# Two 16-head attentions: softmax sums on DVE, sharing on POOL, transposes of whole 128-column chunks

## The reference

```python
# first layer (A): 16 heads of 16, keys and values from the 77 context tokens
e = exp(s - max(s)); p = e / (exp(-m) * 0 + 1.0 + sum(e))     # softmax_one: one more column of weight 1
x = x + tanh(g_xattn[0]) * ((p @ v).heads_joined @ Wp + bp)
# second layer (B): a feed-forward whose two weight matrices are first quantised
scale = max(abs(w)) / 127
wq = clip(round(w / scale), -128, 127) * scale;  w = w + (wq - w)
# seventh layer (G): the same attention, with a bias per head, query and key, and a key mask
attn = q @ k.T * scale + bias;  attn = where(mask, -inf, attn)
x = x + tanh(g_xattn[3]) * ((softmax(attn) @ v).heads_joined @ o_w + o_b)
```

## Time and profile before

| what | value |
|---|---|
| median of 3 runs | 1403.33 us (1400.31 to 1404.64) |
| profiled execution, its own time | 1398.52 us |
| its span, first to last instruction | 1396.5 us |
| PE busy | 1121.6 us (80%) |
| DVE busy | 819.8 us (59%) |
| ACT busy | 580.9 us (42%) |
| POOL busy | 314.9 us (23%) |
| mean granted PE clock | 0.886 of full |

### The profile page before, as it was taken

One profiled execution on the slowest core, in us unless ns is written; L12 is line 12 of the kernel. 1 busy time (PEld: TensorE's weight loads), 2 busy tenths in 40 slices (PEclk: granted clock), 3 DMA queues, 4 the chain that ended last, 5 costly groups with the idle time before them and its releaser, 6 DMA issues.

```text
span 1396.5 us, 22604 instructions
## 1 busy us (share of the span) xinstructions
PE 1121.6 (80%) x8519; PEld 844.9 (60%) x8519; DVE 819.8 (59%) x2107; ACT 580.9 (42%) x1448; POOL 314.9 (23%) x283
## 2 busy tenths in 40 slices
PE   4998799986989897957998899997888752996730
PEld 3666588884447545734666788884666731785530
DVE  5899722248558467972636764556888450552463
ACT  2665433342448535712415313225898440342210
POOL 0009134200435103420010000000000036435266
PEclk9899899995899899988999999997999655898775
DMA  9300054400000003000000720001221023444253
GB/s 316 129 2 2 19 160 131 125 1 0 1 0 2 1 1 121 2 12 12 1 23 2 202 90 1 0 1 37 74 74 38 24 84 105 135 136 115 92 152 118
DMA packets 59841, 88.74 MB, mean 64 GB/s; under 512 B 21315, under 2 KB 50749, under 8 KB 56925
## 3 DMA queue, kind: packets, MB, share of 16 engines
q1 hardware_dynamic: 52301, 67.05, 14.8%
q0 software_dynamic: 7440, 20.33, 5.3%
HBM read 60.60 MB, written 26.76 MB: 63 GB/s over the span
## 4 chain that ended last, share of the span: by engine, by line
PE 52%; DVE 19%; issue 11%; ACT 8%; POOL 4%; another core or an unknown queue 4%; DMA 1%; SPq 0%; POOLq 0%; DVEq 0%; ACTq 0%
PE ps L2571 5%; PE ps L1405 4%; PE ps L1939 4%; PE ps L800 4%; PE ps L813 4%; ACT work L487 2%; POOL pack_F L2830 2%; PE ps L2585 2%; PE ps L1950 2%; PE ps L380 2%; DVE dpack L1731 1%; PE ps L366 1%; DVE work L628 1%; ACT work L494 1%
## 5 line engine op out<-in xcount | busy, mean ns | idle before, releaser
L2822 POOL DMA_INDIRECT hall<-hall_rows,tile_idx x47 | 44.7, 950 | 381.0 <-DVE tile_idx L2728 328.2
L2571 PE MATMUL ps<-big,work 128*128 x316 | 89.2, 408 | 24.9 <-ACT work L2629 16.3
L1905 POOL TENSOR_TENSOR work<-work 128x512 f32<-128x512 f32 x64 | 65.1, 1039 | 143.6 <-DVE work L1753 143.6
L380 PE MATMUL ps<-work,hall 78*32 78x128 f32 (+1 forms) x2048 | 71.7, 282 | 17.4 <-ACT work L494 15.9
L2732 DVE TENSOR_TENSOR work<-work,ps 128x128 f32<-128x128 f32 x79 | 22.9, 290 | 106.4 <-ACT work L2633 51.0
L366 PE MATMUL ps<-pack_const,work 128*78 128x128 f32 (+1 forms) x512 | 73.8, 290 | 9.1 <-DVEq L593 9.1
L2571 PEld LDWEIGHTS ps<-big,work 128*128 128x128 f32 x316 | 58.1, 205 | 32.6 <-issue 27.4
L380 PEld LDWEIGHTS ps<-work,hall 78*32 78x32 f32 (+1 forms) x2048 | 53.9, 112 | 38.5 <-ACT work L494 33.2
L628 DVE RECIPROCAL work<-ps 128x128 f32<-128x128 f32 x64 | 60.8, 950 | 24.8 <-PE ps L380 24.8
L1855 ACT ACTIVATE work<-ps,work 128x256 f32<-128x256 f32 x128 | 58.9, 476 | 38.0 <-DVE work L1748 37.9
L487 ACT ACTIVATE work<-work 128x77 f32<-128x77 f32 x256 | 67.3, 347 | 14.3 <-DVE work L615 13.5
(11 more groups left out here) (515 smaller groups left out, 2644.9 us busy)
## 6 DMA issues: line engine op xcount, KB each, us to landing
expert_rows<-work SPq DMA_DIRECT2D x39, 256.0 KB
masked_bias<-hall SPq DMA_DIRECT2D x8, 1232.0 KB, 5.2
dpack<-masked_bias SPq DMA_DIRECT2D x8, 1232.0 KB, 6.2
hall<-in_fside SPq DMA_DIRECT2D x8, 616.0 KB, 7.4
dpack<-in_pack_D SPq DMA_DIRECT2D x1, 4115.0 KB, 15.7
big<-in_w SPq DMA_DIRECT2D x4, 1024.0 KB, 11.9
big<-in_pack_B SPq DMA_DIRECT2D x1, 2052.0 KB, 10.3
pack_F<-in_pack_F SPq DMA_DIRECT2D x1, 2052.0 KB, 22.4
```

What stands on the lines that cost most here:

```text
L380: mm = nc.tensor.matmul(ps[j * HB32:(j + 1) * HB32, 4, half:half + P], lhsT, A["pT"][0:SK[L], u % 2, h * P:(h + 1) * P], start=g == 0, sto ...
L2571: mm = nc.tensor.matmul(ps[:, GU_B[j % 2], 0:2 * INTER], MW["xT"][:, j % 2, c * P:(c + 1) * P], big[:, bass.ds(at + c * 2 * INTER, 2 * INT ...
```

## The change

The order of work is now given by round g, 0 to 17, in all lists; k = 2g + c counts units. Part by part:

- **Sums on DVE.** `weigh_sum(k)` sums the weights of each head over the free axis (128x8 out of 624 in A, 616 in G) and takes the reciprocal of the eight sums. `normalise` goes, and with it the 128x128 reciprocal and the product on DVE, and half of the matmuls of `weigh_v`, those with the ones.
- **Shares on POOL.** A new list `heads16_pool`: `share(k)` multiplies the weights by the reciprocals. In G `below_max(k)` subtracts the maximum on POOL, so that ACT can do all eight heads in one exponential. `add_bias(g)` adds gate times bias to x on POOL, once for each tile, and `update` on DVE keeps two instructions, with the projection read from PSUM.
- **Flat transposes.** The 624 or 616 weights of a unit are turned in five chunks of up to 128 columns, without regard to heads. The values are laid out to match (`vflat`, eight blocks): at the start PE spreads them with 16 products against shifted copies of the identity (`spread_values`), and DVE copies two banks of PSUM (`take_spread`). `take_pT` copies 640 columns; ACT copies the output to SBUF (`take_o`).
- **Order.** Queries, scores and q are done half by half. DVE takes the first unit's sum ahead of the update of x.
- **Quantisation.** POOL does the two maxima over partitions in round 6 (`ffn_scale_pool`), between the second share of that round and its bias. From round 9 on, each round has one of eight parts of 512 columns: three scalings (`ffn_round_pool`) and two products (`ffn_error_pool`), five instructions in place of six. `ffn_max_dve` stands in rounds 4 and 5 of DVE, `ffn_inv_dve` in round 8.
- POOL's mask work for G, which was behind the quantisation, is now behind all of A's list. D's semaphores have other names.

The core of the diff; its first loop over g is PE's list:

```diff
-            def weigh_v(i, u):
-                for half in (0, D):
-                    for g in range(2):
-                        for j in range(HPG):
-                            lhsT = KV["count"][0:SK[L], b, g, :] if half else KV["vpad"][0:SK[L], b, c * HPC + h, :]
...
+            def turn_p(k, xs):
+                pe.wait_ge(s("pn_ready"), k + 1 + done(L, "pn_ready"))
...
+                for r in range(NCHUNK):
+                    n = chunk_rows(L, r)
+                    mm = nc.tensor.transpose(ps[0:n, PT_BANK + r // 4, r % 4 * P:(r % 4 + 1) * P],
+                                             flat_weights(L, k)[:, r * P:r * P + n], ident)
...
+            def weigh_v(k):
...
+                for e in range(2):
+                    for j in range(HPG):
+                        r, g = VBLOCKS[2 * j + e]
+                        n = chunk_rows(L, r)
+                        mm = nc.tensor.matmul(ps[g * HB32:(g + 1) * HB32, 4, 0:P], KV["vflat"][0:n, 2 * j + e, m, :],
+                                              A["pT"][0:n, k % 2, r * P:(r + 1) * P], start=e == 0, stop=e == 1,
...
+            for g in range(NG16 + 2):
+                if n < HT:
+                    queries(n, co)
+                if g >= 2:
+                    weigh_v(2 * (g - 2) + 1)
+                if 1 <= g <= NG16:
+                    turn_p(2 * (g - 1), min(2 + g // 2, HT))
+                if g >= 2:
+                    project(g - 2)
+                if g % 2 and n + 1 < HT:
+                    turn_x(n + 1)
+                if 1 <= g <= NG16:
+                    weigh_v(2 * (g - 1))
+                if g + 1 < NG16:
+                    scores(g + 1)
+                if 1 <= g <= NG16:
+                    turn_p(2 * (g - 1) + 1, min(2 + (g + 1) // 2, HT))
...
+            def exps(k):
...
+                else:
+                    act.wait_ge(s("below_ready"), k + 1)
+                    nc.scalar.activation(p, sub, ACT.Exp).then_inc(s("p_ready"), 1)
```

The loop of POOL's list:

```diff
+            for g in range(NG16 + 1):
+                if g:
+                    share(2 * (g - 1))
+                if L == "A" and g >= QUANT_AT:
+                    ffn_round_pool(pool, g - QUANT_AT)
+                if L == "G" and g < NG16:
+                    below_max(2 * g)
+                if g:
+                    share(2 * (g - 1) + 1)
+                if L == "A" and g == QUANT_AT - 3:
+                    ffn_scale_pool(pool)
+                if L == "A" and g >= QUANT_AT:
+                    ffn_error_pool(pool, g - QUANT_AT)
+                if L == "G" and g < NG16:
+                    below_max(2 * g + 1)
+                if g < NG16:
+                    add_bias(g)
```

The loop of DVE's list:

```diff
+            for g in range(NG16 + 2):
+                if g < NG16:
+                    shift(g, 0)
+                if 1 <= g <= NG16:
+                    weigh_sum(2 * (g - 1) + 1)
+                if g < NG16:
+                    shift(g, 1)
+                if L == "A" and g in (QUANT_AT - 5, QUANT_AT - 4):
+                    ffn_max_dve(dve, g - QUANT_AT + 5)
+                if L == "A" and g == QUANT_AT - 1:
+                    ffn_inv_dve(dve)
+                if g < NG16:
+                    weigh_sum(2 * g)
+                if g >= 2:
+                    update(g - 2)
```

More of the change, by code:

```diff
@@ L349, in scores @@
+            def scores(g):
+                n, b = divmod(g, B)
+                if b == 0:
+                    pe.wait_ge(s("q_ready"), nth(n, 2, 1) + done(L, "q_ready"))
+                if g < 2:
+                    pe.wait_ge(s("kv_ready"), (2, 5)[g] + done(L, "kv_ready"))
+                if g:
+                    pe.wait_ge(s("sub_ready"), 2 * g + done(L, "sub_ready"))
+                for c in range(DC):
+                    at = c * HPT * SC
                     for j in range(S_TILES):
@@ L398, in heads16_pe @@
+            keys_ctx()
             if L == "G":
@@ new lines, in take_values, with take_spread @@
+                v = ve.tensor_tensor(vs, ps[0:SC, CTXV_BANK, :].rearrange("p (b n) -> p b n", b=B), bv, ALU.add)
+                if L == "G":
+                    for b in range(B):
+                        link(v)
+                        v = ve.tensor_scalar(vs[:, b, :], vs[:, b, :], keep[:, b:b + 1], None, ALU.mult)
+                v.then_inc(s("kv_ready"), 1)
+            def take_spread(part):
+                dve.wait_ge(s("kv_ps"), 3 + part + done(L, "kv_ps"))
+                half = KV["vflat"][:, part * NVB // 2:(part + 1) * NVB // 2].rearrange("p k m e -> p (k m e)")
+                ve.tensor_copy(half, ps[:, (CTXV_BANK, CTXK_BANK)[part], :]).then_inc(s("kv_ready"), 1)
```

485 lines of the change are left out of this document (237 added, 248 removed), and 12 rows, old and new, of the table TOTALS.

## The result

The changed kernel takes 1407.01 us in the median of 20 runs, the kernel before 1396.06 in 20 runs beside it: a ratio of 1.0071, 95% interval 1.0053 to 1.009. That is some 10 us slower, where the prediction had 10 us faster (the medians themselves differ by 10.95). The time lies in the predicted range, the sign is wrong.

The account below looks back on a forecast made before the run. The prediction took DVE as full in A, PE nearly so, and ACT as G's bound. G -29 and A +19 (-6 +30 -3 -2) gave -10: 1398.5 to about 1388.5 us profiled, 1393 as median, range 1376 to 1414.

Parts of the forecast that it names:

- Term G: Attention G: 14 full rounds fall from 8.05 to 6.2 us; with start and tail, -29 us.
- Term A, start and rounds without quantisation: Attention A: rounds 2 to 8 save 8 us, the two first rounds cost +2; -6 us.
- Term A, POOL's scaling and its half-clock round: A's round 6: the maxima block POOL 28 us, 27.5 showing, then PE at half clock costs +2.5; +30 us.
- Term A, rounds 9 to 15 and the tail: End of A: seven POOL-bound rounds of 7.5 us give -3 us, a tail of some 10 us for 12 gives -2.
- Three scalings: 0.49 by a quarter of 1.97, up to 0.65: POOL in A's quantisation rounds: three scalings on 512 columns take 0.49 us each, at most 0.65; 1.9 together with gaps.
- the load in front is free: Rival for A's round 6: POOL fetches the code while waiting or working, so the block is 15 us; 1380, chance 0.20.
- Rounds stuck at 7.2: Rival for G and A: hand-overs between engines do not fit, G saves 14 us less; 1407, chance 0.10.
- Clock: Rival for A's rounds 9 to 16: PE's clock falls to 1.2 GHz, PE becomes the bound, +23 us; 1416, chance 0.20.
- Reciprocals that wait for POOL: Rival for G and A: DVE's small reciprocals each wait 0.65 us for POOL, +27 us; 1420, chance 0.04.

Follow-up runs that it names:

- e2: The changed kernel without the two maxima over partitions, each partition taking its own maximum; ratio 0.9889 to the kernel before, A's length 129.0 us.
- e1: The changed kernel with each part's three POOL scalings written as the four of the kernel before, on 512 columns; ratio 0.996 to the kernel before.
- e12: The changed kernel with 12 useless PE products a round in A's rounds 9 to 16; clock 1.00 for 0.74, A's length unchanged at 155.1 us.
- e3: The changed kernel with both maxima over partitions directly behind each other and both scalings after them; A's length 142.3 us, -12.8.

## Why the prediction was wrong

By its own steps, differences to the kernel before in us:

| step | predicted | measured |
|---|---|---|
| Term G | -29 | -34.8 |
| Term A, start and rounds without quantisation | -6 | -12.2 |
| Term A, POOL's scaling and its half-clock round | +30 | +26.2 (e2) |
| Term A, rounds 9 to 15 and the tail | -5 | +24.2 |
| net of A and G | -10 | +3.4 |

The row of rounds 9 to 15 begins at the eighth update, the scaling is priced by e2, and the row of the start is what remains of A's 38.2 us. Before, the distances between the first seven updates were 11.4 to 11.8 and 4.0 us in turn, so the split depends on the mark: taken at DVE's subtraction for the first unit of round 9 (100.34 us before, 117.77 after), rounds 9 to 15 and the tail are +20.8, and the start and the other rounds -8.8.

**The step that failed** is "Three scalings: 0.49 by a quarter of 1.97, up to 0.65", in the term "rounds 9 to 15, -3 us". It took the price of one pair of operations on 2048 columns, divided it by four, and used it for two pairs that the kernel before does not have on POOL. One of the three was indeed 0.69; the others were 1.93 and 2.00. With the gaps between them the three cost 4.9 us a round (149.62 to 154.52), not 1.9. The rest of the miss is small: products of 1.27 for 1.14, the bias addition 0.72 for 0.55. Together that is 10.66 for 7.5, 3.2 us in each of eight rounds, 25 of the 29 us by which this row of the table is off. Another 1.7 us is the tail: from the end of the last share to the end of A 5.9 us pass, not the 4.2 of the prediction, with a granted clock of 0.64 from 192 to 204 us (the last projection took 2.08 us, one at full clock 1.03). The rest is a matter of the mark. e1 alone gives back 14.9 of it by spelling the same arithmetic differently.

Could it have been seen? Not the size, but the width. The trace of before had one POOL scaling by another pair (subtract+multiply, scalars from two columns), in a later stage; its group:

```profile
L2089 POOL TENSOR_SCALAR hall<-x,mean,route 128x256 f32<-128x256 f32 x16 | 19.3, 1221 | 101.6 <-DVE route L1667 101.6
```

1.22 us on 256 columns is five times L744's price for a column. By that row two scalings could cost 2.4 us each, and the term's upper bound would have been 25 us higher in seven rounds, 29 in eight. I bounded a cost that depends on the operation by a row of one pair of operations only.

**Term A, the scaling**, was right in kind and nearly in size: 26.2 us by e2, for 30. The block lasted 26.4 us, of which 25.0 show (the sixth update comes 30.97 us behind the fifth for 5.95). The next round took 8.73 us, and 7.28 in e2, which has no block: the 1.45 us between are all that PE's half clock can have cost, not 2.5 (granted 0.50 from 101 to 105 us and 0.69 to 110; in e2 1.00 in the rounds at 80 to 90 us). The prediction's sum has a slip too: 13.4 + 13.9 + 1.2 is 28.5, not 28. The load in front, which no row of before showed alone, is 5.75 and 5.83 us, not the 6.7 taken from the way back. The Trainium skill, GPSIMD Engine Reference, section 2.1 (Instruction dispatch), gives 5.95 for it and by it a term of 28.5. The trace agrees (5.75 and 5.83), and the page was nearer than my row. The rival "the load in front is free" is out.

**Term A, the rounds without quantisation**, came out better: a bare round is 5.95 us, under the 6.2 taken, which over seven rounds is 1.8 us. The start cost nothing visible, where I had put +2: the first update comes 2.2 us earlier than before (48.26 for 50.48). **Term G** the same: 14 rounds at 5.95 save 29.4 in place of 26, and start and tail 5.4 in place of 3. DVE's sum of prices, 6.05, would have been the better forecast without the allowance for gaps; half of the 0.10 us that it lies over 5.95 is the update, at 0.43 us in place of 0.48.

**The rivals.** Rounds stuck at 7.2: out, they are 5.95. Clock: its first half came true (0.74 from 128 to 192 us), its second did not, since PE never became the bound (e12). Reciprocals that wait for POOL: out; all 64 of them take 0.20 us, beside 64 shares. The update that stalled 3.19 us behind POOL's product now takes 0.43 to 0.48 with its second input in PSUM, as I had expected.

**Chances.** "Slower" got 0.25, and 0.21 of that stood on the clock and the reciprocals. The right sign came from a cause that had no rival of its own: the bounds given for POOL in a quantisation round were 6.9 and 7.75 us, and it took 10.66. And that 1407 us lies between 1376 and 1414 is luck: the quantisation's row is off by +29.2 us, the three other rows by -15.8 together.

## What to carry to other kernels

When an instruction changes its operations, its price is a new unknown, even where engine, operand kinds and shape stay: bound it by every row of that engine and opcode, not by the one it replaces. On POOL, fewer instructions are not less work if the merged pair is one without the fast form. And work that was free on an idle engine gets its full price on the day that engine enters the chain: here a maximum over partitions that nobody waited for became 26 us, and at most 0.9 us once PE and DVE did it.

## What the runs showed of the hardware

All figures here are for f32. POOL's tensor_scalar has a fast and a slow price, by its pair of operations. On 512 columns multiply+add, add+multiply, multiply+multiply and minimum+maximum take 0.61 to 0.76 us; add+minimum, maximum+multiply, multiply+maximum, subtract+multiply, add+add, multiply+subtract and minimum+minimum take 1.93 to 2.15, a single multiply or maximum 1.50. Add+minimum on 1024 columns takes 3.63, so it goes by the column. Scalars from columns add 0.04 to 0.14 us in either form. The Trainium skill, GPSIMD Engine Reference, section 4.1 (Engine selection), calls one-input work on this engine roughly line-rate. The runs agree for the four fast pairs only (0.62 us on 512 columns is 1.2 ns a column, 1.94 is 3.8).

Changing POOL between ordinary instructions and the maximum over partitions costs 5.55 to 5.83 us going in and 6.73 to 7.06 coming back; a second maximum directly behind the first costs only its own 0.4 us (e3).

Chips differ: the same kernel before takes 1394 to 1399 us on the chips of two sets and 1330 on those of the other two. It was profiled on one chip only; in the traces of the changed kernel and its variants the stage behind G takes 286 to 288 us on the first and 224 on the second. Why is open.
